# Transposing through the DMA queue instead of TensorE in a two-layer graph-attention kernel, with the q and k stack transfers issued by ScalarE

## The reference

```
# layer 0, per sample
q, k, v0 = x @ wq, x @ wk, x @ weight
alpha = softmax(relu(q @ k.T) * (adj != 0), axis=1)
y = layernorm(x + alpha @ v0)
# layer 1, per sample, 16 heads of 32
q, k, v = y @ Wq + bq, y @ Wk + bk, y @ Wv + bv
p = softmax(where(adj == 0, -inf, q_h @ k_h.T * scale))
out = layernorm(y + concat_h(p @ v_h) @ Wo + bo)
```

## Time and profile before

| | |
|---|---|
| runs: median (lowest to highest of 3) | 2967.58 us (2967.09 to 2967.93) |
| span of the profiled execution | 2967.6 us |
| PE busy | 2902.2 us (98%), 24264 matmuls |
| DVE busy | 2365.3 us (80%) |
| ACT busy | 2016.6 us (68%) |
| POOL busy | 582.6 us (20%) |
| DMA engines, mean of 16 | 23.3% for the DMAs that the kernel issues |

### The profile page before, as it was taken

How to read it: one execution, slowest core, us unless ns; L and a number is a source line. 1 busy time by engine, 2 the same in 40 slices (tenths; PEclk the granted TensorE clock), 3 DMA queues, 4 the chain that set the end, 5 groups by cost and what they waited for, 6 DMA issues and landing times. The chain is left out here.

```text
span 2967.6 us, 65967 instructions
## 1 busy us (share of the span) xinstructions
PE 2902.2 (98%) x24264; PEld 1775.5 (60%) x24264; DVE 2365.3 (80%) x4627; ACT 2016.6 (68%) x6414; POOL 582.6 (20%) x1289
## 2 busy tenths in 40 slices
PE   7899999999999999999999999999999999999996
PEld 4565666656666656666666666666666666666554
DVE  4588888888888788888788888888888888888886
ACT  3476676666676766676767766767776766776665
POOL 1121122121122121121121221121221211221210
PEclk9999999999999999999999999999999999999997
DMA  3222122222122222122221122221122221222220
GB/s 121 61 72 76 43 56 73 57 76 72 37 65 61 69 76 62 40 72 54 76 76 54 48 72 54 76 76 47 51 76 54 76 76 42 57 71 59 75 53 24
DMA packets 96369, 188.06 MB, mean 63 GB/s; under 512 B 18608, under 2 KB 34992, under 8 KB 96048
## 3 DMA queue, kind: packets, MB, share of 16 engines
q1 hardware_dynamic: 96048, 183.84, 23.3%
HBM read 49.55 MB, written 33.55 MB: 28 GB/s over the span
## 5 line engine op out<-in xcount | busy, mean ns | idle before, releaser
L647 ACT ACTIVATE e<-sm,nmax 128x128 f32<-128x128 f32 x2048 | 791.1, 391 | 27.6 <-DVE nmax L776 25.6
L598 ACT ACTIVATE qk<-front,bqk 128x512 f16<-128x512 f32 x256 | 175.9, 687 | 381.6 <-PE front L429 381.6
L825 POOL TENSOR_TENSOR ln<-ln 128x1 f32<-128x1 f32 x256 | 49.0, 192 | 1890.2 <-DVE ln L804 1496.6
L647 ACT ACTIVATION_READ_ACCUMULATOR e<-sm,nmax 128x1 f32 x2048 | 391.0, 191 | 0.0
L664 DVE SCALAR_TENSOR_TENSOR pT<-pt_bank,pT 128x512 f16<-128x512 f32 x512 | 348.9, 681 | 42.6 <-ACT pT L653 42.1
L653 ACT ACTIVATE pT<-pt_bank 128x512 f16<-128x512 f32 x512 | 302.8, 591 | 103.6 <-PE pt_bank L543 101.6
L776 DVE TENSOR_REDUCE nmax<-sm 128x4 f32<-128x512 f32 x512 | 351.3, 686 | 17.7
L429 PE MATMUL fin_bank<-W_O,oT 128*128 128x512 f16 x1536 | 356.3, 382 | 1.4 <-DVE oT L664 1.4
L429 PE MATMUL front<-W_V,yT 128*128 128x512 f16 x1536 | 354.0, 380 | 0.0
L429 PE MATMUL front<-xT,W_A 128*128 128x512 f16 x1536 | 353.6, 380 | 0.3 <-DVE xT L664 0.3
L429 PE MATMUL front<-yT,W_Q 128*128 128x512 f16 x1536 | 352.2, 379 | 1.6 <-DVE yT L664 1.6
(11 more groups left out here) (111 smaller groups left out, 4482.3 us busy)
## 6 DMA issues: line engine op xcount, KB each, us to landing
q_st<-qk SPq DMA_DIRECT2D x384, 128.0 KB, 2.4
k_st<-qk SPq DMA_DIRECT2D x384, 128.0 KB, 2.4
x_sb<-in_x SPq DMA_DIRECT2D x128, 256.0 KB, 3.4
out_x<-z_sb SPq DMA_DIRECT2D x128, 256.0 KB, 2.5
adj_i<-in_adj SPq DMA_DIRECT2D x32, 256.0 KB, 4.6
y_sb<-in_L_gnn_wq SPq DMA_DIRECT2D x1, 1024.0 KB, 5.6
yb<-in_L_gnn_wk SPq DMA_DIRECT2D x1, 1024.0 KB, 8.1
x_p<-in_L_gnn_weight SPq DMA_DIRECT2D x1, 1024.0 KB, 10.5
```

The source lines that it names most:

```text
L598: i = act.activation(dst, src, ACT.Identity, bias=bias, scale=scale)
L647: act.activation(e1[:, k % 2, h, :], sm[:, k % SM_BUFS, h, :], ACT.Exp, bias=nmax[:, k % SM_BUFS, h:h + 1], accum_out=esum[:, n % 2, head: ...
L825: pool.tensor_tensor(ln[:, 8:9], ln[:, 7:8], ln[:, 8:9], ALU.add).then_inc(moments, 1)
```

## The change

All transposes leave PE. What is to be transposed is first split in SBUF, where it lies: `x_parts` (HI by ACT, LO now by DVE), `y_parts` and `o_parts` (new: HI by ACT, LO by POOL), `P` (the probabilities, HI by ACT, LO by DVE). Then SP issues one DMA transpose that takes HI and LO together, 128 partitions by 1024 float16 values (256 KB), from SBUF to SBUF: 4 for x, 4 for y, 16 for the probabilities and 4 for the outputs in each group, and one of 128 by 512 for the adjacency. The 24 stack transfers are issued from ACT's queue (steps `stack_q` and `stack_k`, three transfers a step). PSUM banks that come free become a fourth front bank and a second score bank. The order of steps is a new list, `PASS`, with the age of each step beside it; `PT_BUFS` = 4 transposed probability buffers and `P_BUFS` = 2 split ones are kept. Scale factors move along, and the epsilon is no longer set by a DVE memset.

```diff
-        ("xT", 0), ("xT", 1), ("x_parts", 0), ("xT", 2), ("PV", 14), ("adj01", 0), ("pT", 15), ("xT", 3), ("v", 2),
...
+PASS = [
+    ("adj01", 0, 0), ("t", 3, 0), ("P", 15, 2), ("stack_k", 2, 1), ("stack_k", 3, 1), ("pT", 14, 2), ("fin", 1, 2),
+    ("alpha", 0, 0), ("alpha", 1, 0), ("p0", 0, 0), ("adjT", 0, 0), ("oT", 2, 2), ("p0", 1, 0), ("pT", 15, 2), ("oT", 3, 2),
+    ("o", 3, 2), ("v", 0, 1), ("PV", 12, 2), ("o_parts", 3, 2), ("PV", 13, 2), ("PV", 14, 2), ("PV", 15, 2), ("S", 0, 1),
+    ("S", 1, 1), ("z", 0, 0), ("z", 1, 0), ("residual1", 1, 1), ("norm1", 1, 2), ("fin", 2, 2), ("exp", 0, 1), ("P", 0, 1),
...
+    ("stack_q", 2, 0), ("k", 2, 0), ("t", 0, -1), ("k", 3, 0), ("xT", 2, -1), ("stack_q", 3, 0), ("xT", 3, -1), ("t", 1, -1),
+    ("stack_k", 0, 0), ("t", 2, -1), ("mask", 0, 0), ("stack_k", 1, 0), ("pT", 13, 1),
+]
...
-        fbank = [ps(f"front{i}") for i in range(3)]
-        s_bank, pt_bank, pv_bank, ot_bank, fin_bank = (ps(n) for n in ("s_bank", "pt_bank", "pv_bank", "ot_bank", "fin_bank"))
+        fbank = [ps(f"front{i}") for i in range(4)]
+        s_bank = [ps(f"s_bank{i}") for i in range(2)]
+        pv_bank, fin_bank = (ps(n) for n in ("pv_bank", "fin_bank"))
...
+                elif what == "xT":
+                    sp.wait_ge(xlo_ready, count(g, GB, k + 1))
+                    sp.dma_start_transpose(xT[:, k, :, :, :].rearrange("p a t n -> p (a t) n"),
+                                           parts[:, k, :, :].rearrange("p a d -> p (a d)")).then_inc(xT_turned, 16)
+                elif what == "adjT":
+                    sp.wait_ge(adj01_ready, g + 1)
+                    sp.dma_start_transpose(adjT[:, :, :], adj01[:, :, :].rearrange("p b m -> p (b m)")).then_inc(adjT_turned, 16)
...
+                elif what == "pT":
+                    sp.wait_ge(plo_ready, count(g, STEPS, k + 1))
+                    wait(sp, pv_done, count(g, STEPS, k + 1 - PT_BUFS))
+                    sp.dma_start_transpose(pT[:, k % PT_BUFS, :, :, :].rearrange("p a h n -> p (a h) n"),
+                                           p_p[:, k % P_BUFS, :, :].rearrange("p a m -> p (a m)")).then_inc(pT_turned[k % PT_BUFS], 16)
+                elif what == "oT":
+                    sp.wait_ge(olo_ready, count(g, GB, k + 1))
+                    wait(sp, fin_full, count(g, GB, k))
+                    sp.dma_start_transpose(oT[:, :, :, :].rearrange("p a t n -> p (a t) n"),
+                                           o_p[:, :, :].rearrange("p a d -> p (a d)")).then_inc(oT_turned, 16)
...
-                if what == "xT":
-                    if k == 0:
-                        pe.wait_ge(x_loaded, count(g, 16 * GB, 16 * GB))
-                    bank = bank_for(g)
-                    for n in range(GB):
-                        mm = pe.transpose(bank[:, n * P:(n + 1) * P], x_sb[:, n, k * P:(k + 1) * P], ident[:, :])
-                    mm.then_inc(f_full, 1)
...
+                if what == "t":
+                    if k == 0:
+                        pe.wait_ge(xT_turned, count(g, 16 * GB, 16 * GB))
...
+                elif what in ("stack_q", "stack_k"):
+                    n = int(what == "stack_k")
+                    dst, split_as = ((q_st, (HI, LO, HI)), (k_st, (HI, HI, LO)))[n]
+                    if k == 0:
+                        act.wait_ge(f_free, jobs_done(g, "qk"[n], KT - 1))
+                        wait(act, s_full, count(g, STEPS, 0))
+                    for row, part in enumerate(split_as):
+                        act.dma_start(dst[row * DH:(row + 1) * DH, k, :, :],
+                                     qk[k * DH:(k + 1) * DH, n, part, :, :]).then_inc(stacked[n], 16)
...
+                elif what == "P":
+                    act.wait_ge(exp_done, count(g, 4 * STEPS, 4 * (k + 1)))
+                    n = count(g, STEPS, k) - P_BUFS
+                    if n >= 0:
+                        act.wait_ge(pT_turned[n % PT_BUFS], 16 * (n // PT_BUFS + 1))
+                    act.activation(p_p[:, k % P_BUFS, HI, :], e1[:, k % 2, :, :].rearrange("p h m -> p (h m)"),
+                                   ACT.Copy, scale=P1_SCALE).then_inc(phi_ready, 1)
```

More of the change, by code:

```diff
@@ L54 @@
 SM_BUFS = 4
+P_BUFS = 2
+PT_BUFS = 4
 STACK_DMAS = 3 * 4
[L57 to L68, removed]
[18 rows of a table removed]
[L93 to L109, removed]
@@ L112, in order @@
[L112 to L135, removed]
@@ L161, in graph_layers, with schedule, count @@
+FRONT_JOBS = ("t", "alpha", "z", "g", "q", "k", "v")
+HI_JOBS = ("t", "z", "q", "k", "v")
+def schedule(groups):
+    ages = [age for _, _, age in PASS]
+    return [(what, k, p - age) for p in range(min(ages), groups + max(ages)) for what, k, age in PASS if 0 <= p - age < groups]
+def count(g, per_group, k):
+    return g * per_group + k
 def graph_layers(nc, x, adj, w0, wq0, wk0, wq, bq, wk, bk, wv, bv, wo, bo, out):
     groups = x.shape[0] // GB
+    steps = schedule(groups)
+    job_at = {step: n for n, step in enumerate(s for s in steps if s[0] in FRONT_JOBS)}
+    hi_at = {step: n for n, step in enumerate(s for s in steps if s[0] in HI_JOBS)}
@@ L297, in wait @@
                 eng.wait_ge(s, value)
[L299 to L321, removed]
@@ L323, in jobs_done, with run_steps @@
-        def jobs_done(at, *job):
-            return job_number(at, job) + 1
-        def his_done(at, *job):
-            return job_number(at, job, HI_JOBS) + 1
-        def front_bank(at, *job):
-            assert len(JOBS) % len(fbank) == 0
-            place = (None, 0) if is_at(at, 0) else (None, groups) if is_at(at, groups) else (None, 1)
-            return fbank[job_number(place, job) % len(fbank)]
-        def v_pass(g, k):
-            return before(g, -age("v", k))
-        def raw(parts):
-            return parts.bitcast(F32).rearrange("p (t o) -> p t o", t=KT)
+        def run_steps(step):
+            for what, k, g in steps:
+                step(what, k, g)
@@ L367, in _ @@
             sp.dma_start(bo_all[:, :], bo.rearrange("(a d) -> a d", a=1).to_broadcast([P, D])).then_inc(bias_loaded, 16)
-            def load(g):
-                if not is_at(g, 0):
-                    sp.wait_ge(f_free, jobs_done(before(g, 1), "g", GB - 1))
-                for b in range(GB):
-                    src = x_d[g[1] if g[0] is None else g[0]]
-                    sp.dma_start(x_sb[:, b, :], src[b, :, :]).then_inc(x_loaded, 16)
-                wait(sp, adj01_ready, count(g, 1, 0))
-                src = adj_d[g[1] if g[0] is None else g[0]]
-                sp.dma_start(adj_i[:, :, :], src).then_inc(adj_loaded, 16)
@@ L381, in stack @@
-            def stack(n, f):
-                dst, parts = ((q_st, (HI, LO, HI)), (k_st, (HI, HI, LO)))[n]
-                sp.wait_ge(f_free, jobs_done(f, "qk"[n], KT - 1))
-                wait(sp, s_full, count(f, STEPS, 0))
-                for r in range(4):
-                    for row, part in enumerate(parts):
-                        sp.dma_start(dst[row * DH:(row + 1) * DH, r, :, :],
-                                     qk[r * DH:(r + 1) * DH, n, part, :, :]).then_inc(stacked[n], 16)
@@ L391, in store @@
-            def store(b, g):
-                sp.wait_ge(out_ready, count(g, GB, b + 1))
-                dst = out_d[g[1]] if g[0] is None else out_d[g[0] + g[1]]
-                sp.dma_start(dst[b, :, :], z_sb[:, b % 2, :]).then_inc(out_stored[b % 2], 16)
-            steps = [w for w in pass_order() if w[0] in ("norm1", "stack", "load_next")]
-            cut = steps.index(("load_next", 0))
-            def run(these, at, ages=(0, 1, 2)):
-                for what, k in these:
-                    if age(what, k) in ages and what == "stack":
-                        stack(k, at)
-                    elif age(what, k) in ages:
-                        store(k, before(at, age(what, k)))
@@ L421, in _ @@
+            run_steps(step)
             for n in range(2):
```

277 lines of the change are left out of this document (124 added, 153 removed), and 33 rows, old and new, of tables (LATE_ATTENTION, PASS).

## The result

The changed kernel takes 3163.81 us (median of 4 runs, 3154.05 to 3177.83) against 2967.58 us before: 1.0663 times as long, 95% interval 1.0636 to 1.069. One of the ten runs of experiment 7 fell into a slower state, 3603.2 us at a granted clock of 0.784, and its ratio leaves that run out.

What follows compares the result with a forecast made beforehand. PE was taken to bound the kernel before; after the change a loop through SP's transposes and t0, summed to 96.4 us a pass, gives 32 x 96.4 + 110 = 3195, say 3200 us; range 2700 to 4050, the forecast's own 2980 to 3620.

Steps and rivals of the forecast that it cites:

- What PE gains: On PE, dropping the transposes saves 12.5 us a pass, leaving 76.8 us of work.
- 1.6 us a pass for the clock: On PE, the gap in front of t0 lowers TensorE's clock, adding 1.6 us to the loop.
- T: Time one 256 KB DMA transpose keeps SP's stream, taken as 2.45 us; slower than before above 2.15 us.
- byte end: Lower bound for one transpose on SP's queue: it moves at the stacks' 175 GB/s, 1.50 us.
- block end: Upper bound for one transpose on SP's queue: eight 128 x 128 blocks, each costing an issue, 3.46 us.
- The line through two row lengths: DMA cost by row, from 85 and 58 ns: 54 ns for 256 bytes, 3.4 us a transpose.
- 37.6 + 24 T: Length in us of the loop through SP's transposes and PE's t0 that sets a pass; 96.4 us forecast.
- rival A: On SP's queue, transposes go at their byte rate, 1.50 us each; PE stays the bound, 2730 us; chance 0.34.
- Landing of xT, 1.8 us: Between SP's last xT issue and PE's t0, the transfer needs 1.8 us to land.
- SP's wait for P: On SP's queue, pT0 to pT4 wait for the probabilities from ACT, estimated at 4 us a pass.
- The wait of oT for the output projection: On SP's queue, oT3 waits 7.3 us for fin2, growing 2.5 us for each us that T falls.
- What would show it: Signs on SP and PE: queue nearly full, transposes about 2.4 us, PE waiting at t0 and q0, busy near 80%.

Runs made afterwards that it cites:

- experiment 7: Kernel before the change, plus 28 DMA transposes of 256 KB a pass on SP's queue that nobody reads: 2975.4 us, ratio 1.0025.
- Experiment 2: Changed kernel, each stack transfer copying only one of its four slices, the rest zero: 2918.7 us, ratio 0.9838 to the kernel before.
- Experiment 8: Changed kernel, LO half of the probabilities computed for only 32 of 512 columns, the rest zero: 3077.9 us, ratio 1.0365 to the kernel before.
- experiment 1: Changed kernel with the 24 stack transfers issued from SP's queue again instead of ACT's: 3282.2 us, ratio 1.1061 to the kernel before.

## Why the prediction came out

The time was right, 3200 against 3163.8 us, and so was the sign. The price at its heart was not: two errors of opposite sign and nearly the same size met, and that they did is luck.

**What PE gains** held. PE was to keep 32 x 12.5 = 400 us less; it is busy 249 us less. Of the missing 151 us, 127 are two groups that ran partly at the lower clock: t0 to t3 take 403.6 us against 353.6, the output projection 433.1 against 356.3. The other 24 are not placed. The prediction had 1.6 us a pass for the clock, one gap; these two groups are 4.0, since the middle has gaps too:

```profile
1407.23 0.61 PE L423 MATMUL s_bank<-k_st,q_st 96*128 96x128 f16 x4 [3.43 <-DVE sm L646]
...
1409.54 4.99 PE L337 MATMUL fin_bank<-W_O,oT 128*128 128x512 f16 x12
```

The granted clock from 1409.5 to 1414.5 us is 0.54.

**T was too large.** It was chosen as 2.45 us, the middle between the byte end of 1.50 and the block end of 3.46. It is 1.51 back to back in experiment 7. In the change itself: between the adjacency loads at 90.97 and 2945.46 us, 30 passes apart, SP's waits are 1404.5 us, 46.8 a pass; a pass is (2945.46 - 90.97) / 30 = 95.15 us; less 4.7 us of plain issues that leaves 43.6 us for 28.5 transposes, 1.53 each. The line through two row lengths from HBM gave the block end its weight, and rows within SBUF were the nearer ones: both source and target of the stacks lie where those of a transpose do. The line was also read too high. The store issued at 1319.70 us ends in the window of the loads, which moved 158 GB/s for 9 us, 1422 KB, where the loads are 1311; without it an adjacency row is 49 ns and not 58, and the block end by rows 2.8 us and not 3.4 (estimates). The byte end has a flaw too: the stacks' 175 GB/s were read at a DMA share of 0.77, with the engines not full, so that it met the 1.51 us of the transposes is in part chance. Taking the middle between the two was the step that failed.

**By its own loop, 37.6 + 24 T, this was rival A**: 73.6 us of loop at T = 1.50, 82 us a pass, 2730 us. Waits that were too small or left out made up for the 24 us that T had too much (26.5 x 0.92). In the mean of 28 passes of the trace the stretch from the issue of adjT to the end of that of xT3 takes 73.5 us against 80.0 predicted, from there to t0 6.7 against 1.8, and from t0 to the next adjT 15.2 against 14.6: 95.4 against 96.4. What was missing, term by term:

- *Landing of xT, 1.8 us.* In the pass shown it is 7.5 us, in the mean 6.7, from the end of the last xT issue at 1339.53 to t0 at 1347.00. The prediction costed the stacks on ACT only as issues, 14.2 us of ACT's time, and never asked what their bytes would run beside. Experiment 2 prices the stacks' bytes at 7.7 us a pass, with the clock behind the gap, the waits for pT and ACT's stalls in it.
- *SP's wait for P, "an estimate of 4 us".* It is 584.2 / 32 = 18.3 us. The probabilities come late because DVE is full in the middle, and the LO half was left at its old length when it moved from PSUM to SBUF, where POOL stretches it. Experiment 8 takes (584.2 - 429.7) / 32 = 4.8 us a pass off this wait, and 2.7 off the time; how the rest splits between DVE, the two buffers of p_p and the order was not measured.
- *Waits for the output parts and for x.* Left out; 47.7 / 32 = 1.5 and, less the 15.2 of the setup, 1.8 us.

The wait of oT for the output projection was 7.3 us, to grow by 2.5 for each us that T falls: 9.7 at 1.5 us. It is 322.2 / 32 = 10.1. These shares of waits are taken over the whole run and partly lie outside the loop, so with the other terms they add up to some 3 us more than a mean pass. The pass that the rows show, 1264.08 to 1362.99, is a long one: 75.5 for SP's part, 7.5 for landing and 16.0 from t0 on, 98.9 us in all. The mean pass is 95.15 against 96.4, and outside the passes there are 107 us against 110.

**What would show it.** PE busy near 80%: 84%. PE waiting on xT at t0: yes, 231.0 us, but at q0 on yT hardly (9.5). SP's queue nearly full with transposes of 2.4 us: wrong, it waits for half of each pass. The sign that was to decide, the median transpose on SP's queue, is 1.27 us and pointed to A, whose time did not come, for A's working had the same short waits as the forecast's. The sign named for another outcome, short issues with a landing of many us, is what the page shows for x. ACT as the bound: no, it is busy 62%, and without the stack issues (experiment 1) the kernel only gets slower. DVE 68.4 us a pass: 71.3, the surplus of 2.9 being the stretched LO halves (512 x 0.22 us / 32 = 3.5).

So the forecast of a loop through SP's queue and t0 was right in its place, and its size came from waiting and collisions where the working had transfer time. One slip of arithmetic stands beside this: at T = 2.15 the loop's own formula gives 32 x 89.2 + 110 = 2964 us and not 2980 for the lower end of the forecast's own range.

## What to carry to other kernels

Moving a transpose from a full engine to a DMA trades work for latency: price the path from the producer through the queue, the landing and the clock behind the gap to the consumer, and take the steps with the shortest slack off the list first (here the probabilities, whose return to PE, with another order and other banks, gave 0.966). A second issuing queue saves the issues' time and the waits at the head of the first, and no time of the DMA engines, so ask what its bytes will run beside. And when a VectorE step's operand moves from PSUM to SBUF, look at what POOL runs at that time.

## What the runs showed that was not expected

- A DMA transpose of 256 KB within SBUF keeps its queue 1.23 us at least (xT: 1231 ns) and 1.51 us when seven run back to back, and lands after 2.8 us when alone; beside the q stack its issue took up to 3.55 us and its landing up to 12.2.
- Issued seven ahead of each store, 28 of them a pass cost a full kernel 0.25% at a DMA share of 0.75. Three quarters of the stacks' bytes, for which PE does wait, cost 245 us.
- The same VectorE step on 128x512 with both inputs in SBUF took 0.66 us alone and 1.76 behind a POOL tensor_tensor; 36% of these steps met one.
- After 10.17 us without work, 12 matmuls of PE took 5.30 us instead of 2.75; after a gap of 3.43 us and another of 0.99 us in the middle of the pass they took 4.99 us.
